# Moving two layout changes of a fused attention and expert kernel from TensorE transposes to VectorE blocks and DRAM copies

## The reference

```python
mixed = silu(causal_conv(hidden @ w_qkv, conv_w))      # 4 taps
q, k, v = split(mixed)                                 # z = hidden @ w_z
def step(state, xs):                                   # over 512 rows
    state = state * exp(g_t)
    kv = k_t @ state
    state = state + outer(k_t, (v_t - kv) * b_t)
    return state, q_t @ state
o = outs * silu(z)
o = o * rsqrt(mean(o * o) + EPS) * norm_gamma
x = layernorm(x + o.reshape(B, S, 4096) @ w_out)
x = layernorm(x + moe(rmsnorm(x)))                     # 8 experts, top 2, one shared
```

## Time and profile before

| | |
|---|---|
| Time, median of 3 runs | 2248.97 us (2248.55 to 2250.84) |
| Profiled execution: its own time | 2250.69 us |
| Span of its trace | 2249.0 us |
| TensorE busy | 2185.4 us (97%) |
| VectorE busy | 1807.9 us (80%) |
| ScalarE busy | 1207.0 us (54%) |
| GpSimd busy | 1173.4 us (52%) |
| DMA queue of SyncE, share of 16 engines | 38.8% |

### The profile page before, as it was taken

One profiled execution on the slowest core, in us unless ns is written; L12 is line 12 of the kernel. 1 busy time (PEld: TensorE's weight loads), 2 busy tenths in 40 slices (PEclk: granted clock), 3 DMA queues, 4 the chain that ended last, 5 costly groups with the idle time before them and its releaser, 6 DMA issues.

```text
span 2249.0 us, 49842 instructions
## 1 busy us (share of the span) xinstructions
PE 2185.4 (97%) x17998; PEld 1734.1 (77%) x17998; DVE 1807.9 (80%) x3299; ACT 1207.0 (54%) x3869; POOL 1173.4 (52%) x1193
## 2 busy tenths in 40 slices
PE   6899999999999999999999999999999999989998
PEld 3687888878888878888888878778888888876665
DVE  5788888888888888888888888888888888874665
ACT  4555555556555556555566655565555565542110
POOL 3455656555656555665555656556565556541000
PEclk9999999999999999999999999999999999999999
DMA  3544444434434344434344444444444343341000
GB/s 112 112 86 100 90 108 82 106 79 94 110 82 108 86 99 92 109 81 110 85 81 111 93 97 92 102 83 109 89 101 88 83 109 90 81 93 47 28 10 19
DMA packets 437604, 198.92 MB, mean 88 GB/s; under 512 B 409840, under 2 KB 415344, under 8 KB 437104
## 3 DMA queue, kind: packets, MB, share of 16 engines
q1 hardware_dynamic: 437360, 195.73, 38.8%
HBM read 92.39 MB, written 2.62 MB: 42 GB/s over the span
## 4 chain that ended last, share of the span: by engine, by line
PE 91%; DMA 5%; DVE 2%; ACT 1%; issue 1%; POOLq 0%; POOL 0%; DVEq 0%; SPq 0%; ACTq 0%
PE bank L992 19%; PE bank L1134 10%; PE bank L1019 8%; PE bank L550 5%; PE bank L1089 5%; PE bank L1116 5%; PE bank L1034 5%; DMA XT<-X 4%; PE bank L1115 4%; PE bank L1077 4%; PE bank L1051 4%; PE bank L1043 4%; PE bank L1099 4%; PE bank L1124 3%; PE bank L1002 3%; PE bank L566 3%
## 5 line engine op out<-in xcount | busy, mean ns | idle before, releaser
L1288 DVE SCALAR_TENSOR_TENSOR conv<-bank,cw_all,conv 128x511 f32<-128x511 f32 (+2 forms) x768 | 565.8, 744 | 83.6 <-ACT conv L1182 74.5
L992 PE MATMUL bank<-xT,w_kh 128*128 128x512 f32 x1024 | 519.0, 599 | 0.4 <-ACT sqj L1205 0.4
L1228 ACT ACTIVATE X<-bank 128x512 f16<-128x512 f32 x384 | 230.7, 601 | 232.4 <-PE bank L1051 227.4
L1182 ACT ACTIVATE conv<-bank,cw_all 128x512 f32<-128x512 f32 x256 | 179.0, 699 | 256.6 <-PE bank L992 256.5
L1319 DVE TENSOR_TENSOR N<-bank,lev 128x512 f16<-128x512 f32 x384 | 261.9, 682 | 35.7 <-PE bank L1043 28.4
L921 POOL TENSOR_SCALAR_AFFINE_SELECT mhiT<-m32T 128x512 f16<-128x512 f32 x128 | 81.9, 640 | 376.3 <-DVE m32T L1300 376.2
L1134 PE MATMUL bank<-wo,ogT 128*128 128x256 f32 x1024 | 264.7, 381 | 0.7 <-ACT ogT L1246 0.7
L1019 PE MATMUL bank<-w_kh,xT 128*128 128x256 f32 x1024 | 243.4, 381 | 0.0
L1019 PEld LDWEIGHTS bank<-w_kh,xT 128*128 128x128 f32 x1024 | 186.1, 191 | 54.9 <-issue 30.1
L1134 PEld LDWEIGHTS bank<-wo,ogT 128*128 128x128 f32 x1024 | 185.7, 192 | 47.8 <-issue 30.1
L1233 ACT ACTIVATE U<-bank 128x256 f32<-128x256 f32 x256 | 100.7, 393 | 184.9 <-PE bank L1089 184.8
(11 more groups left out here) (176 smaller groups left out, 5268.3 us busy)
## 6 DMA issues: line engine op xcount, KB each, us to landing
egb<-rows SPq DMA_DIRECT2D x64, 512.0 KB, 4.0
ecb<-rows SPq DMA_DIRECT2D x64, 512.0 KB, 4.1
w_kh<-w_heads SPq DMA_DIRECT2D x16, 768.0 KB, 4.6
XT<-X SPq DMA_TRANSPOSE x384, 3.1
wo_raw<-w_out SPq DMA_DIRECT2D x16, 256.0 KB, 4.7
xT<-x_cols SPq DMA_DIRECT2D x4, 512.0 KB, 5.5
xT<-gate_up SPq DMA_DIRECT2D x1, 2048.0 KB, 8.1
ecb<-x_rows SPq DMA_DIRECT2D x3, 512.0 KB, 4.1
```

Of the source, the lines that this page charges most:

```text
L992: mm = pe.matmul(PB[j % 2][:, :], w[:, k, g * P:(g + 1) * P], xT[:, k, b * SEQ:(b + 1) * SEQ], start=(k == 0), stop=(k == KT - 1))
L1182: act.activation(conv[:, g, :], PB[i % 2][:, :], ACT.Copy, scale=cw_all[:, head, g * TAPS + 3:g * TAPS + 4]).then_inc(s_tap, 1)
L1228: act.activation(blocks(X[:, p], i, 0), packed(IB[p], i), ACT.Copy).then_inc(s_x[p], 1)
L1288: dve.scalar_tensor_tensor(conv[:, g, m:], PB[j % 2][:, 0:SEQ - m], cw_all[:, head, g * TAPS + 3 - m:g * TAPS + 4 - m], conv[:, g, m:], op ...
```

## The change

Four things change, and the order of the pieces with them.

1. v. `vtp` and its 8 transposes go. `vt` (VectorE) turns `vT` in blocks of 32 x 32 into the two v rows of `conv`; `vst` (SyncE) writes these 512 KB to DRAM; `vld` (SyncE) reads them back in four DMAs of 32 partitions each, into the place of `vT`, so that blocks land where a whole transpose would put them. `vals` (ScalarE) now reads SBUF instead of PSUM.
2. The gated output. `turn` goes on TensorE (8 transposes) and on ScalarE (two copies from PSUM). `ot` (VectorE) turns `og` in 32 x 32 blocks into `og2`, `ost` and `old` (SyncE) move it through DRAM into `ogT`. The cells lie interleaved there: `ot` writes with a step of 8 elements, and `project` reads its weights with that step.
3. `x0` is no longer a VectorE transpose but a DMA transpose from `XT` to `X` on SyncE.
4. `join` 5 goes from VectorE to ScalarE, which copies rows 64 to 127 of the product to a new tile `last_N`; its upper half is filled with the identity once. `last_N` has one buffer, so the copy waits for `growx` 5 of the body before.

```diff
     "sync": [
-        ("ecs", 0, 1), ("flip", 5, 0), ("flip", 0, 1), ("flip", 1, 1), ("egs", 0, 3), ("flip", 2, 1), ("flip", 3, 1),
-        ("flip", 4, 1), ("weights", 0, 2),
+        ("flip", 5, 1), ("flip", 0, 2), ("vst", 0, 2), ("flip", 1, 2), ("vld", 0, 2), ("egs", 0, 4), ("ost", 0, 0),
+        ("flip", 2, 2), ("old", 0, 0), ("ecs", 0, 3), ("flip", 3, 2), ("flip", 4, 2), ("x0", 0, 3), ("weights", 0, 2),
     ],
...
+            def load_blocks(dst, src, n, loaded):
+                blocks_of = src[n % 2].rearrange("(a s) (b k) -> b s a k", a=Q32, b=Q32)
+                for b in range(Q32):
+                    sp.dma_start(dst[32 * b:32 * b + 32], blocks_of[b]).then_inc(loaded[n % 2], 16)
...
+                elif name == "x0":
+                    p = n % 2
+                    sp.wait_ge(s_pair, 2 * n + 2)
+                    if n > 1:
+                        sp.wait_ge(s_resp, 2 * (n - 1))
+                    sp.dma_start_transpose(X[:, p], XT[:, p].rearrange("p a n -> p (a n)")).then_inc(s_x0[p], 16)
+                elif name == "vst":
+                    sp.wait_ge(s_vt, n + 1)
+                    sp.dma_start(v_blocks[n % 2], flat(conv[:, 2:4])).then_inc(s_vst[n % 2], 16)
+                elif name == "vld":
+                    sp.wait_ge(s_vst[n % 2], 16 * (n // 2 + 1))
+                    load_blocks(vn.rearrange("p a x r -> p a (x r)"), v_blocks, n, s_vld)
+                elif name == "ost":
+                    sp.wait_ge(s_ot, n + 1)
+                    sp.dma_start(o_blocks[n % 2], flat(og2)).then_inc(s_ost[n % 2], 16)
+                elif name == "old":
+                    sp.wait_ge(s_ost[n % 2], 16 * (n // 2 + 1))
+                    if n > 0:
+                        sp.wait_ge(s_opp, 2 * n)
+                    load_blocks(ogT4, o_blocks, n, s_old)
...
                 elif name == "project":
...
                     h, c = divmod(i, 2)
-                    if c == 0:
-                        pe.wait_ge(s_gt, n * 2 + h + 1)
+                    if i == 0:
+                        pe.wait_ge(s_old[p], 16 * Q32 * (n // 2 + 1))
                     for v in range(VH):
-                        mm = pe.matmul(OB[h][:, 256 * c:256 * c + 256], ogT[:, 2 * i + v, :], wo[:, head % 2, v, :],
+                        mm = pe.matmul(OB[h][:, 256 * c:256 * c + 256], flat(ogT)[:, 2 * i + v::CELLS], wo[:, head % 2, v, :],
                                        start=(v == 0), stop=(v == VH - 1))
...
                 elif name == "vals":
-                    act.wait_ge(s_vtp, n * 2 + i + 1)
+                    act.wait_ge(s_vld[p], 16 * Q32 * (n // 2 + 1))
...
+                elif name == "join":
+                    act.wait_ge(s_np[p], level(n, i))
+                    if n > 0:
+                        act.wait_ge(s_xgp[1 - p], level(n - 1, i))
+                    act.activation(last_N[64:, :, :], packed(IB[p], i)[64:, :, 0], ACT.Copy).then_inc(s_n[p], 1)
...
+                elif name == "ot":
+                    dve.wait_ge(s_on, 2 * n + 2)
+                    dve.transpose(flat(og2).rearrange("p (b s x) -> p b x s", b=Q32, x=CELLS),
+                                  flat(og).rearrange("p (x b s) -> p b x s", b=Q32, s=32)).then_inc(s_ot, 1)
+                elif name == "vt":
+                    dve.wait_ge(s_silu, 4 * n + 4)
+                    dve.transpose(flat(conv[:, 2:4]).rearrange("p (b x s) -> p b x s", b=Q32, s=32),
+                                  flat(vT).rearrange("p (x b s) -> p b x s", b=Q32, s=32)).then_inc(s_vt, 1)
```

116 lines of the change are left out of this document (55 added, 61 removed).

## The result

| | median us | runs | span of the profiled execution | granted clock |
|---|---|---|---|---|
| before | 2248.76 | 2247.1 to 2250.84 | 2249.0 | 1.00 in the steady stretch |
| changed | 2420.23 | 2419.66 to 2421.85 | 2418.8 | 1.00 in the steady stretch |

The ratio is 1.0763, with a 95% interval of 1.0745 to 1.0782: the changed kernel is 7.6% slower, where 3.1% faster was forecast. Against the page of before, the page of the changed kernel shows what share of the span each engine is busy, and the chain that ended last.

What follows compares the result with a forecast made beforehand. TensorE, busy 97%, was taken as the bound: 28.35 us of matmul + 0.2 + 0.75 of new waits = 29.3 us a round, 1.25 less. Over 62.5 rounds -78 us, +8 outside, gave 2179 us; range 2124 to 2270.

Steps and rivals of the forecast that it cites:

- the sum of new waits: TensorE, per round: waits added by the new order, mainly for flips 2 and 3, put at 0.75 us.
- `project` is the same matmuls with stepped weights, taken at no cost: TensorE, `project`: loads of fp32 weights run beside matmuls, so reading them with a step adds 0 us.
- the fourth: Rival at `project` on TensorE: stepped weight loads over twice as long add 1.6 us a round, 2279 us; chance 0.05.
- I take 1.24: VectorE: each fp32 block transpose, `vt` and `ot`, takes 1.24 us, the lower bound; upper bound twice that.
- So flip 2 lands at about 21.3, 0.2 late: SyncE: flip 2, issued at 17.9 behind the 512 KB `ost`, lands 0.2 us late.
- flip 3 0.7 late: SyncE: behind `old` and `ecs`, flip 3 lands at about 27.3 us; `growx` 4 wants it at 26.6.
- the 0.2 us of before: TensorE: the part of a round that is not matmul, 0.2 us, kept unchanged for the new order.
- nothing covers them today: TensorE: the 16 removed transposes, 1.98 us a round, are saved in full, from 30.35 to 28.35 us of matmul.
- 21 of 28.35 us: DMA engines: busy time per round after four moves and the crossbar `x0` add 7.8 us to 13.1.
- held flips: Rival at SyncE's queue: slow quarter loads delay flips 2 and 3, 3.6 us of waits a round, 2357 us; chance 0.17.
- The full gain: Rival for the whole round: the order absorbs the new waits, 28.55 us a round, 2132 us; chance 0.26.
- VectorE as the bound: Rival on VectorE: both transposes at 2.5 us, round about 30.4 us, 2248 us, no change; chance 0.1.

Runs made afterwards that it cites:

- e1: Changed kernel with `ot` writing runs of 32 and `project` reading contiguous weights (no steps, wrong elements multiplied); 2383.99 us, ratio 1.061.
- e2: Changed kernel with all ten DMAs kept but moving only 32 of 256 elements of each piece; 2291.17 us, ratio 1.0196.
- e6: Changed kernel with both small moves (32 of 256 elements) and no 8-element steps in `ot` and `project`; 2240.32 us, ratio 0.9955.
- k3: Kernel before with only v going through VectorE blocks and DRAM, and the `ecs` load one round earlier behind `vst`; 2225.2 us, ratio 0.9897.
- b1: Kernel before with only `x0` moved from VectorE to a crossbar DMA behind flip 4; 2287.73 us, ratio 1.0174.
- a1: Changed kernel with `x0` back on VectorE between the last `conv` and `og` 0, order otherwise as changed; 2429.88 us, ratio 1.0779.
- k2: Kernel before with only v going through VectorE blocks and DRAM, `x0` staying on VectorE; 2242.24 us, ratio 0.9968.
- e3: Changed kernel with decay loads earlier on SyncE: `ecs` behind flip 5, `egs` behind `vst`; 2335.68 us, ratio 1.038.
- e9: Changed kernel with `egs` behind flip 3, `ecs` behind `x0` and the weights behind `vst` on SyncE; 2320.21 us, ratio 1.0316.

## Why the prediction was wrong, step by step

The forecast round was 29.3 us, 28.35 of matmul, 0.2 as before and 0.75 of new waits. It is 33.2. The step that failed is the sum of new waits, 0.75 us, with flips 2 and 3 at its centre; a second, smaller one is the term that was put at nothing, stepped weights. By the table above, waits went from 0.9 to 4.8 us, 3.9 more. 2.3 of these are at `growx`, 0.5 each at `write` and `project`, 0.4 at `read`. The matmuls fell by 1.8 us with the transposes (forecast 1.98) and rose by 0.35 with the steps: 30.8 - 1.8 + 0.35 + 3.9 = 33.2.

- **"`project` is the same matmuls with stepped weights, taken at no cost" failed.** The loads went from 190 to 333 ns, and from one record of `project` to the next it is 240 ns instead of 216; both pieces of a round together cost 0.47 us more. I had judged that loads hide beside matmuls of 0.215 us distance as long as they take less than twice as long; at 1.75 times they are no longer hidden. The Trainium skill (SBUF — State Buffer, Door 1: The DMA port swizzle, on 16-byte lines) says that fp32 is free up to a step of 4 elements and that beyond it accesses pay. The runs agree, at a step of 8: 1.75 times for a weight load, 1.67 for a block transpose's write. As a rival (the fourth) this had 0.05, and was priced at 1.6 us a round, three times what it was.
- **VectorE: "I take 1.24" for both transposes** was right for `vt` (1.245) and wrong for `ot` (2.058, near the upper bound of 2.5, by the reason that I had named for it). VectorE did not become the bound: it is busy 975 of 1180 us. But `ot` ended at 1024.89, 18.7 us behind `join` 5 (1006.17), instead of 17.4, and flip 2 was issued 19.1 behind it, instead of 17.9. It also held `s` 1 and so `read`, by 0.45 us a round, near the "few tenths" that I had named; e1 gives them back.
- **"So flip 2 lands at about 21.3, 0.2 late", and flip 3 0.7 late: this failed, and it is the main term.** The places are right: TensorE's first wait of the steady stretch is for a flip, twice a round, at `growx` 3 and 4. The sizes are not. In the round shown flip 2 landed at 23.0, 3.87 us from its issue, 0.5 more than I had, and flip 3 at 29.5, 5.28 after its issue; the medians are worse, 4.5 and 5.4. `ecs`, whose landing I put at the 4.0 us of a quiet queue, "at the earliest", and then worked with, takes 5.0; `old` is still in flight when it is issued. Together 2.3 us a round at `growx` (0.8 with small moves, e2). Nor did my own list add up to the sum: 0.2, 0.7 and the few tenths at `read` are more than the 0.75 that I put.
- **The rest of the order, put at the 0.2 us of before, failed.** I took the old order's near absence of waits for a property of the engine's load. It was one of the old order. The new one still has 2.5 us of waits a round, against 0.9, when the moves carry an eighth of their bytes and nothing is stepped (e6): `growx` 0.9, `write` for U 0.5, and many pieces of some 0.1. How much of the 0.9 is the order and how much `ecs` ahead of flip 3 no run tells apart. The same fault stands in "nothing covers them today" of the 16 transposes. Nothing ran on TensorE beside them, true, but they themselves covered `x0` on VectorE and a copy of ScalarE; k3 gained 0.3 to 0.4 us a round for eight transposes, and by the table 0.65 came back as waits at these two places.
- **DMA: "21 of 28.35 us", a share of 0.74.** The share is 0.71 of a longer round, 23.6 us. By the shares, four moves and `x0` cost 10.4 us of the engines over the 13.2 of before (0.43 x 30.79), not 7.8: `v`'s two 3.8 (k3: 0.56 x 30.37), `x0` 1.8 (b1: 0.48 x 31.37), which leaves 4.8 for the output's two. The share itself misled: what counts is that it is 1.0 for 5.7 us around flip 3 and 0.00 right behind it.
- **`x0` "lands some 1.5 us before `join` 0"**: this held (2.1 us in the median), and in the changed kernel nothing was to be gained by taking it back (a1). "The weights' rounds cost what they cost now" did no harm either: rounds with weights are no longer than the others (33.11 against 33.25). On the old order the crossbar `x0` cost 1.7% (b1).
- **Outside the rounds: +8** was forecast. 8.4 comes out if all 63 distances count as rounds, 23.9 if the last, 46.75 us long, counts as the end. So the agreement hangs on where one cuts, and I can't claim it.
- **The rivals.** The first, held flips, named the place and the waits above 1.8 us, with 0.17. Its price, 3.6 us at flips 2 and 3, is near the 3.9 of all new waits, but that is luck: only 2.3 stand there, and its 2357 us are 63 short of the measured time. Its cause, loads by quarters at half rate, is not what was seen. They land 3.0 to 3.1 us after their issue, about as the whole store of `v` does (3.0), and `vst`'s and `vld`'s part of the change does not cost anything (k2). The Trainium skill (SBUF — State Buffer, Door 1: The DMA port swizzle) has 32 partitions reach half the ports; these runs do not tell a rate for one quarter alone, since four are in flight together, and nothing in them needs the rule: moving the decay loads alone (e3) gave back 1.3 us a round, and with the weights also moved (e9) 1.5. Of its other two signs, `old` landing more than 5 us after its issue came in 12 of 35 rounds (the median, from the first issue to the last landing, is 4.7). The clock did not fall: the granted clock of the steady stretch, in which TensorE is busy 0.92 of the time, is 1.00, so waits cost no clock there. The full gain is out of reach of this order: even e6, at 30.45 us a round, is far from 28.55. VectorE as the bound did not occur.

The range failed because I let the place that rival 1 named depend on one doubtful cause. The two rows at hand, 5.1 us for a flip behind 1.5 MB and 6.9 for the load ahead of it, were for a queue that holds traffic once in four rounds. The change makes that every round, and I used them as the price of the exceptional case only.

## What to carry to other kernels

A DMA that a matmul chain waits for should be priced by what has been issued in the microseconds before it, not by the mean share of the DMA engines: 1 MB issued in the 2.6 us ahead of a flip of 3.1 us made it 5.3 at a mean share of 0.71, and ordering the same bytes differently was worth 100 us. An engine that is busy 97% still has waits of others covered by its own work: before pricing a removed instruction at its full length, look at what becomes ready while it runs (here 0.94 us of transposes covered 0.65 of waits). Price a strided operand from a run of its own if no row shows one. Compare a round's gain with the medians of the times as well: the profiled execution of e1 was 13 us faster than its median.

## What the runs showed of the hardware

- fp32 with a step of 8 elements: a 128x128 weight load takes 333 ns against 190 (e1), a block transpose of 1024 elements that writes so 2058 against 1235 (e1), and eight records of `project` 1.91 and 2.10 us (e2) against 1.73 and 1.81 (e6).
- A block transpose of fp32 takes as long as one of fp16 with the same count (1235 to 1245 ns against 1235).
- DMA engines that were busy all the time moved 250 GB/s in one stretch, and 151 in the next, where flip 3 was among it: the share tells that they are busy, not what they move.
- A crossbar transpose of 256 KB landed 3.1 us after its issue in a quiet queue, 4.6 behind one 512 KB load and small moves (e6), and 5.4 behind 1 MB (changed).
- An eighth of the bytes in the same ten DMAs, with all waits kept, took 2.0 of 33.2 us off a round (e2): the bytes, not the number of issues, were this price.
